# Conditioned linear-attention layer on one core: the last two turns of a software pipeline put in another order

## The chip, the cores and the metric

The kernel runs on one core of a Trainium2 chip. The metric is the device time of one execution in microseconds, the median of several runs. Names of engines are those of the profile: PE (TensorE, the matrix engine), PEld (its weight loads), DVE (VectorE), ACT (ScalarE), POOL (GpSimd), SP (the queue that issues loads and stores of x). PE writes PSUM only, and POOL works on SBUF only.

## The reference

Input x is 128 sequences of 64 tokens by 256 features in float32; there are 8 heads of 32. The softmax of q runs over a head's features, that of k over the tokens.

```python
xn = _ln(x, ln_w, ln_b)
q = xn @ Wq + bq
k = xn @ Wk + bk + (1.0 - src_mask) * -1000000.0
q = softmax(q.reshape(b, t, h, dh), axis=-1)
k = softmax(k.reshape(b, t, h, dh), axis=1)
v = ((xn @ Wv + bv) * src_mask).reshape(b, t, h, dh)
att = jnp.einsum('bnhd,bnhl->bhdl', k, v)
y = jnp.einsum('bnhd,bhdl->bnhl', q, att).reshape(b, t, d)
scale, shift = jnp.split((silu(emb) @ W_emb + b_emb)[:, None, :], 2, axis=2)
hh = _ln(y, ln2_w, ln2_b) * (1.0 + scale) + shift
hh = silu(hh) @ W_out + b_out
return x + hh
```

## The kernel before

The 8192 tokens are worked in G = 16 groups of 512 tokens (T = 4 tiles of 128 tokens, GB = 8 sequences). The features are C = 2 chunks of 128. Large products are split in float32r parts, high times high, high times low and low times high.

Each engine runs its own list of turns, `steps(engine, body)`: i = -1, 0, 1, 2 written out, the turns up to 14 in a hardware loop of two turns, and i = 15, 16, 17 written out. In turn i the engines work at up to four groups at once, by flags: N, the statistics and layer norm of x of group i+1; F, "front", K, Q and V of group i; B, attention and y of group i-1; O, the output of group i-2. Turn 15 has F, B, O; turn 16 has B (group 15) and O (group 14); turn 17 has only O (group 15). Within an engine, instructions start in the order of its list. Between engines, semaphores order them: each stage counts one up (`k_d`, `att_d`, `y_d`, `yhat_d`, ...), and who needs it waits for a count.

The steps of one group, with the lines of the profile:

- ACT's exp k (L400); PE transposes exp k into the banks `be` (L715, `exp_k_transposed`); ACT copies them to `e_k` (L389).
- ACT's exp q (L396); PE transposes it into the banks `bt` (L766); ACT copies that to `q_t` (L406).
- PE's attention, 128 small matmuls of `e_k` and `v_s` into `be` (L782); DVE's reciprocal of the sums (L596) and `kv` (L600).
- PE's y, 128 small matmuls of `kv` and `q_t` into all four banks of `by` (L802). `be` is banks 0 and 1 of `by`, `bt` its banks 2 and 3.
- DVE: reciprocal `rq` (L627), `y_s` (L631), statistics (L638, L641), two small ones (L644, L645); POOL: the power -0.5 (L340), a product (L342), the normalized y in place in `y_s` (L345; four tiles, in turn 16 two on POOL and two on ACT at L443).
- PE transposes the normalized y into `be` (L725, `y_transposed`); DVE scales it to `z_s` (L556), POOL adds the shift (L236; in turn 17 DVE); ACT's tanh `th` (L412); DVE's `h_s` = (th + 1) z (L609); ACT's rounded copy `h_hi` (L426); POOL's rest `h_lo` (L240; in turn 17 DVE).
- PE's output product, 24 matmuls of 256 columns into `bv` (lines 816 to 825; four of h_hi come before the wait for h_lo); DVE adds it to x (L656), in two halves; SP stores.

The profile gives the helper's line, L665, for all matmuls made by `mm`, so they are told apart by their tiles: `by<-v_s,e_k` is attention, `by<-kv,q_t` is y, `bv<-w_o_hi,h_hi` and its like the output product. In PE's turn 16 the order is: exp k of 15 transposed, y of 14 transposed, q of 15 transposed, attention of 15, y of 15, output product of 14. In turn 17: y of 15 transposed, output product of 15. The banks `bk_` hold K and then tiles 2 and 3 of the Q and V product; nothing writes them after turn 15.

Of the kernel before, what the change touches and what calls it, by code (L numbers as in the profile page):

```python
# [20 lines left out]
def build_layer(nc, x, cond_t, columns_in, b_qvk, mask_rows, wq, wk, wv, w_emb, w_out, b_out, out):  # L21
    fp32 = mybir.dt.float32
    f32r = mybir.dt.float32r
    ALU = mybir.AluOpType
# [3 lines left out]
    P = 128  # L28
# [16 lines left out]
    with ctx:  # L45
# [245 lines left out]
        def _(pool):  # L291
# [8 lines left out]

            def body(i, par, N, F, B, O):
# [149 lines left out]
        def _(dve):  # L451
# [99 lines left out]

            def z_scaled(g):
                for c in range(C):
# [4 lines left out]
                        be[c][:, :].rearrange("p (b s) -> p b s", s=SEQ),  # L558
# [6 lines left out]
            def body(i, par, N, F, B, O):  # L565
                if F:
# [22 lines left out]
                if B:  # L589
                    g = i - 1  # L590
                    wait(dve, att_d, g + 1)
                    wait(dve, kv_d, 2 * g)
                    sums = [be[e][:, 0:GB // 2 * C * AW].rearrange("p (b c n) -> p b c n", c=C, n=AW)
                            for e in range(2)]
                    for e in range(2):
                        nc.vector.reciprocal(rk[:, e, :, :], sums[e][:, :, :, DH]).then_inc(rk_d, 1)  # L596
                    wait(dve, y_d, g)
                    for e in range(2):
                        wait(dve, rk_d, 2 * g + e + 1)
                        nc.vector.tensor_tensor(  # L600
                            kv[:, e:GB:2, :, :], sums[e],
                            rk[:, e, :, :].unsqueeze(3).broadcast_to([P, GB // 2, C, AW]),
                            ALU.mult).then_inc(kv_d, 1)
                if O:
                    g = i - 2
                    for c in range(C):
                        wait(dve, th_d, 2 * g + c + 1)
                        wait(dve, hlo_d, 2 * g)
                        nc.vector.scalar_tensor_tensor(h_s[:, c, :], th[:, c, :], 1.0, z_s[:, c, :],  # L609
                                                       ALU.add, ALU.mult).then_inc(h_d, 1)  # L610
                    if last_step(i):
                        for c in range(C):
                            wait(dve, hhi_d, 2 * g + c + 1)
                            wait(dve, o_d, 2 * g)
                            h_low(nc.vector, c).then_inc(hlo_d, 1)
                if F:
                    q_tiles(i, par, (0, 1))
                if B:
# [44 lines left out]
        def _(pe):  # L663
# [55 lines left out]
            def y_transposed(g, B):  # L719
                wait(pe, yhat_d, 4 * g + 4)  # L720
                for c in range(C):
                    if B:
                        wait(pe, ek_d, 2 * g + c + 3)
                    for t in range(T):
                        last = nc.tensor.transpose(be[c][:, t * P:t * P + P], y_s[:, t, c * P:c * P + P],  # L725
# [3 lines left out]
            def body(i, par, N, F, B, O):  # L729
# [9 lines left out]
                if B:  # L739
                    exp_k_transposed(i - 1, par)  # L740

                for c in range(C):
# [15 lines left out]
                    if O and c == 0:  # L758
# [104 lines left out]
```

## Time and profile before

| | before |
|---|---|
| median of 3 runs | 356.78 us (354.89 to 357.75) |
| the profiled execution | 354.55 us |
| its span, first to last instruction | 352.7 us |
| PE busy | 326.3 us (93%) |
| DVE busy | 280.0 us (79%) |
| POOL busy | 193.3 us (55%) |
| ACT busy | 182.5 us (52%) |
| mean granted PE clock | 0.985 |

Times in the timelines are microseconds from the span's start. A timeline row is one instruction or several alike merged; in brackets stands how long the engine had sat idle before it, and who ended that wait. A PE matmul's time reaches from its start to a modelled end, and consecutive ones overlap, so their rate is read from starts. The granted clock is 1.00 at 2.4 GHz and 0.50 at 1.2 GHz. A steady turn takes about 20 us.

### The profile page before, as it was taken

The page shows a single profiled execution, that of the slowest core. Times are in us where ns is not written, and L with a number is a line of the kernel's source. Part 1 is how long each engine was busy: PE and PEld are TensorE (multiplying, and loading weights), DVE is VectorE, ACT ScalarE, POOL GpSimd, SP SyncE. Part 2 cuts the span into 40 slices and gives each one's busy share as a digit, 9 for nine tenths or more (in the row PEclk, how much of TensorE's full clock was granted, in tenths as well). Part 3 has the DMA queues.
Part 4 walks back from the last instruction along what each step waited for, and adds up shares of the span by engine and source line. Part 5 has one row for each costly group of instructions (what it writes and reads, how often), then busy time and mean ns, then how long its engine had stood idle before and what let it go on. Part 6 is the DMA issues. An engine that isn't in the chain of part 4 may idle for free.

```text
span 352.7 us, 14361 instructions
## 1 busy us (share of the span) xinstructions
PE 326.3 (93%) x5644; PEld 267.9 (76%) x5644; DVE 280.0 (79%) x749; ACT 182.5 (52%) x360; POOL 193.3 (55%) x244
## 2 busy tenths in 40 slices
PE   3799999999999999999999999999999999999736
PEld 2387868888787788788787788888788788888625
DVE  3777879698887969698887969698887969777672
ACT  0537547465455647465445647465545747453340
POOL 1221466467492937567492837567393837556520
PEclk9999999999999999999999999999999999999886
DMA  8920100301203030300203030200303010101011
GB/s 251 226 61 1 63 1 6 115 9 39 84 3 119 0 119 0 109 10 32 87 0 119 0 119 0 85 34 24 95 0 119 0 59 0 62 4 56 8 62 59
DMA packets 19818, 19.75 MB, mean 56 GB/s; under 512 B 1233, under 2 KB 19281, under 8 KB 19794
## 3 DMA queue, kind: packets, MB, share of 16 engines
q1 hardware_dynamic: 18144, 17.96, 16.6%
q10 hardware_dynamic: 1650, 1.45, 1.4%
q8 instruction: 17, 0.28, 0.3%
q14 instruction: 7, 0.06, 0.1%
HBM read 10.95 MB, written 8.39 MB: 55 GB/s over the span
## 4 chain that ended last, share of the span: by engine, by line
PE 47%; POOL 22%; issue 12%; DVE 11%; DMA 4%; DVEq 1%; POOLq 1%; ACT 1%; ACTq 0%
PE bk L665 19%; PE bv L665 14%; POOL h_lo L240 9%; PE by L725 4%; POOL xr L317 4%; PE by L715 3%; PE by L736 3%; POOL x_all L328 3%; PE by L665 3%; DVE kmax L578 3%; POOL xr L319 3%; DMA n_row<-n_lo 2%; DVE xstat L466 2%; POOL y_s L345 1%; DVE xmv L470 1%
## 5 line engine op out<-in xcount | busy, mean ns | idle before, releaser
L236 POOL TENSOR_TENSOR z_s<-z_s,mod_shift 128x512 f32<-128x512 f32 x30 | 30.7, 1044 | 68.7 <-DVE z_s L556 68.7
L400 ACT ACTIVATE k_t<-k_t 128x512 f32<-128x512 f32 x32 | 20.2, 631 | 64.7 <-DVE k_t L582 64.7
L383 ACT ACTIVATE xt_hi<-by 128x512 fp32r<-128x512 f32 x32 | 17.4, 597 | 46.6 <-PE by L736 46.6
L578 DVE TENSOR_REDUCE kmax<-bk 128x8 f32<-128x512 f32 x32 | 22.1, 690 | 23.8 <-PE bk L665 22.5
L240 POOL TENSOR_TENSOR h_lo<-h_s,h_hi 128x512 fp32r<-128x512 f32 x30 | 38.0, 1289 | 4.9 <-ACT h_hi L426 4.9
L665 PE MATMUL bv<-w_o_hi,h_hi 128*128 128x256 f32 x128 | 35.5, 296 | 4.5 <-ACT h_hi L426 4.5
L328 POOL TENSOR_TENSOR x_all<-x_all,bo_all 128x1024 f32 (+1 forms) x16 | 38.2, 2389 | 0.1
L345 POOL TENSOR_SCALAR y_s<-y_s,yr 128x256 f32<-128x256 f32 x62 | 33.9, 563 | 2.6 <-POOL yr L342 2.2
L665 PE MATMUL bv<-w_o_lo,h_hi 128*128 128x256 f32 x128 | 35.1, 294 | 0.0
L665 PE MATMUL bv<-w_o_hi,h_lo 128*128 128x256 f32 x128 | 28.6, 306 | 6.8 <-POOL h_lo L240 6.8
L656 DVE TENSOR_TENSOR x_all<-bv,x_all 128x512 f32 (+1 forms) x32 | 22.1, 691 | 14.9 <-PE bv L665 13.9
L432 ACT ACTIVATE xhat<-x_all,xr 128x256 f32 (+1 forms) x64 | 33.1, 592 | 1.1 <-POOL xr L321 1.1
L315 POOL TENSOR_SCALAR xr<-xmv 128x4 f32<-128x4 f32 x16 | 3.2, 198 | 52.1 <-DVE xmv L470 52.1
L665 PEld LDWEIGHTS bv<-w_o_hi,h_hi 128*128 128x128 f32 x128 | 25.8, 202 | 5.4 <-ACT h_hi L426 4.7
L665 PEld LDWEIGHTS by<-kv,q_t 32*64 32x64 f32 x2048 | 23.8, 131 | 7.7 <-issue 6.4
L665 PE MATMUL bk<-xt_hi,w_k_hi 128*128 128x512 f32 x64 | 28.6, 446 | 0.0
L665 PEld LDWEIGHTS bv<-w_o_hi,h_lo 128*128 128x128 f32 x128 | 21.0, 201 | 9.7 <-POOL h_lo L240 9.7
L665 PE MATMUL by<-kv,q_t 32*64 32x33 f32 x2048 | 25.7, 223 | 1.9 <-DVE kv L600 1.2
L665 PEld LDWEIGHTS bv<-w_o_lo,h_hi 128*128 128x128 f32 x128 | 25.8, 202 | 0.6
L569 DVE TENSOR_TENSOR xt_lo<-by,xt_hi 128x512 fp32r<-128x512 f32 x32 | 20.6, 685 | 6.2 <-ACT xt_hi L383 6.2
L665 PE MATMUL bk<-xt_hi,w_k_lo 128*128 128x512 f32 x64 | 25.3, 396 | 0.0
L582 DVE TENSOR_TENSOR k_t<-bk,kmax 128x512 f32<-128x512 f32 x32 | 22.1, 691 | 2.2
(104 smaller groups left out, 842.2 us busy)
## 6 DMA issues: line engine op xcount, KB each, us to landing
x_all<-in_x SPq DMA_DIRECT2D x16, 512.0 KB, 4.5
out<-x_all SPq DMA_DIRECT2D x15, 512.0 KB, 3.2
z_s<-in_w_emb ACTq DMA_DIRECT2D x1, 512.0 KB, 8.3
h_s<-in_w_emb ACTq DMA_DIRECT2D x1, 512.0 KB, 11.5
out<-x_all SPq DMA_DIRECT2D x2, 256.0 KB, 2.1
y_s<-in_wk SPq DMA_DIRECT2D x1, 256.0 KB, 3.1
q_t<-in_wq SPq DMA_DIRECT2D x1, 256.0 KB, 5.2
th<-in_cond_t ACTq DMA_DIRECT2D x1, 256.0 KB, 6.7
```

What stands on the lines that cost most here:

```text
L236: return eng.tensor_tensor(z, z, mod_shift[:, c, span(g, GB)].unsqueeze(2).broadcast_to([P, GB, SEQ]), ALU.add)
L240: return eng.tensor_tensor(h_lo[:, c, :], h_s[:, c, :], h_hi[:, c, :].bitcast(fp32), ALU.subtract)
L328: nc.gpsimd.tensor_tensor(xg, xg, bo_all[:, :].unsqueeze(1).broadcast_to([P, T, D]), ALU.add).then_inc(xb_d, 1)
L345: nc.gpsimd.tensor_scalar(y_s[:, t, :], y_s[:, t, :], yr[:, 1, t:t + 1], yr[:, 3, t:t + 1], ALU.mult, ALU.add).then_inc(yhat_d, 1)
L383: nc.scalar.activation(xt_hi[:, c, :], bt[c][:, :], ACT.Copy).then_inc(hi_d, 1)
L400: nc.scalar.activation(k_t[:, par, c, :], k_t[:, par, c, :], ACT.Exp).then_inc(kexp_d, 1)
L432: nc.scalar.activation(xhat[:, 1 - par, t, :], group_of(x_all, g)[:, :, t * D:t * D + D].rearrange("p g n -> p (g n)"), ACT.Identity, scal ...
L569: nc.vector.tensor_tensor(xt_lo[:, c, :], bt[c][:, :], xt_hi[:, c, :].bitcast(fp32), ALU.subtract).then_inc(lo_d, 1)
L578: nc.vector.tensor_reduce(out=kmax[:, c, :], in_=kk, axis=AX.X, op=ALU.max).then_inc(kmax_d, 1)
L582: nc.vector.tensor_tensor(k_t[:, par, c, :].rearrange("p (b s) -> p b s", s=SEQ), kk, kmax[:, c, :].unsqueeze(2).broadcast_to([P, GB, SEQ] ...
L656: nc.vector.tensor_tensor(xg, bv_[e][:, :], xg, ALU.add).then_inc(res_d, 1)
L665: return nc.tensor.matmul(dst, lhsT, rhs, start=start, stop=stop)
```

## The change

In the written-out turns 15 and 16 four things change place:

- PE transposes exp k of group 15 in turn 15, behind the Q and V product and ahead of the output product of group 13, in place of the start of turn 16.
- PE transposes y of group 14 behind the attention of group 15 in place of ahead of the q transposes, and into K's banks `bk_`; it waits for the last q_s of turn 15 (`qsub_d`), no longer for the copies of exp k. The attention waits for z_s of group 13 in place of 14.
- DVE does the reciprocals and kv of group 15 (`kv_scaled`) first in turn 16, ahead of z_s of 14; and h_s of group 14 (`h_product`) behind the statistics of y of 15 in place of ahead of the reciprocal of y.
- POOL does h_lo of group 14 (`h_lows`) behind the normalized y of 15 in place of ahead of the power.

The helpers `kv_scaled`, `h_product` and `h_lows` hold, unchanged, the lines that stood in the bodies. In the diff POOL's list comes first, then DVE's, then PE's.

```diff
+        def yt_bank(g):
+            return bk_ if isinstance(g, int) and g == G - 2 else be
...
-                if O and not last_step(i):
-                    g = i - 2
-                    for c in range(C):
-                        wait(pool, hhi_d, 2 * g + c + 1)
-                        wait(pool, o_d, 2 * g)
-                        h_low(nc.gpsimd, c).then_inc(hlo_d, 1)
+                if O and not last_step(i) and not last_y(i):
+                    h_lows(i - 2)
...
                     for t in range(T) if not last_y(i) else (0, 1):
                         nc.gpsimd.tensor_scalar(y_s[:, t, :], y_s[:, t, :], yr[:, 1, t:t + 1], yr[:, 3, t:t + 1],
                                                 ALU.mult, ALU.add).then_inc(yhat_d, 1)
+                if last_y(i):
+                    h_lows(i - 2)
...
-                        be[c][:, :].rearrange("p (b s) -> p b s", s=SEQ),
+                        yt_bank(g)[c][:, :].rearrange("p (b s) -> p b s", s=SEQ),
...
             def body(i, par, N, F, B, O):
+                if last_y(i):
+                    kv_scaled(i - 1, i)
...
+                if B and not last_y(i):
+                    kv_scaled(i - 1, i)
+                if O and not last_y(i):
+                    h_product(i - 2, i)
...
                     nc.vector.tensor_scalar(yr[:, 2, :], ymv[:, :, 0], -1.0, None, ALU.mult).then_inc(yve_d, 1)
+                if last_y(i):
+                    h_product(i - 2, i)
...
             def y_transposed(g, B):
                 wait(pe, yhat_d, 4 * g + 4)
+                if isinstance(g, int) and g == G - 2:
+                    pe.wait_ge(qsub_d, 4 * G)
                 for c in range(C):
-                    if B:
+                    if B and not (isinstance(g, int) and g == G - 2):
                         wait(pe, ek_d, 2 * g + c + 3)
...
-                if B:
+                if B and not last_y(i):
                     exp_k_transposed(i - 1, par)
...
-                    if O and c == 0:
+                    if O and c == 0 and not last_y(i):
                         y_transposed(i - 2, B)
...
-                    wait(pe, zs_d, 2 * g)
+                    wait(pe, zs_d, 2 * g - 2 if last_y(i) else 2 * g)
...
                     last.then_inc(att_d, 1)
+                    if last_y(i):
+                        y_transposed(i - 2, B)
...
                     qv_tile(i, 3)
+                    if isinstance(i, int) and i == G - 1:
+                        exp_k_transposed(i, 1 - par)
```

How the engines' lists stand before and after follows, from the built programs. The line numbers of the changed kernel differ (L715 is L732 there, L725 L744, L766 L785, L665 L682).

PE before, from the last matmuls of the output product of 13 at the end of turn 15 to the first of the output product of 14 in turn 16 (`k_t` is exp k, `v_s,e_k` attention, `kv,q_t` y):

```order
L665 MATMUL bv<-w_o_hi,h_lo 128x256 x2
L715 MATMUL by<-ident,k_t 128x128 x8
L725 MATMUL by<-ident,y_s 128x128 x8
L766 MATMUL by<-ident,q_s 128x128 x8
L665 MATMUL by<-v_s,e_k 32x33 x64
L665 MATMUL by<-kv,q_t 64x33 x64
L665 MATMUL bv<-w_o_hi,h_hi 128x256
```

The same place after:

```order
L682 MATMUL bv<-w_o_hi,h_lo 128x256 x2
L785 MATMUL by<-ident,q_s 128x128 x8
L682 MATMUL by<-v_s,e_k 32x33 x64
L744 MATMUL bk<-ident,y_s 128x128 x8
L682 MATMUL by<-kv,q_t 64x33 x64
L682 MATMUL bv<-w_o_hi,h_hi 128x256
```

The exp k transposes are gone from here (they stand now directly ahead of the output product of 13), and those of y stand between attention and y, into `bk`. Behind this piece nothing moves: the output product of 14 and then the transposes of y of 15.

DVE before, turn 16, from z_s of 14 to the residual of 14 (`rk` and `kv` of 15, `h_s` of 14, then y of 15):

```order
L556 TENSOR_TENSOR z_s<-by,mod_scale 128x512 x2
L596 RECIPROCAL rk<-by 128x8 x2
L600 TENSOR_TENSOR kv<-by,rk 128x4x66 x2
L609 SCALAR_TENSOR_TENSOR h_s<-th,z_s 128x512 x2
L627 RECIPROCAL rq<-by 128x32
L631 TENSOR_TENSOR y_s<-by,rq 128x512 x2
L638 BN_STATS ystat<-y_s 128x6 x4
L641 BN_AGGR ymv<-ystat 128x2 x4
L644 TENSOR_SCALAR yr<-ymv 128x4
L645 TENSOR_SCALAR yr<-ymv 128x4
L656 TENSOR_TENSOR x_all<-bv,x_all 128x512 x2
```

And after:

```order
L567 RECIPROCAL rk<-by 128x8 x2
L571 TENSOR_TENSOR kv<-by,rk 128x4x66 x2
L592 TENSOR_TENSOR z_s<-bk,mod_scale 128x512 x2
L642 RECIPROCAL rq<-by 128x32
L646 TENSOR_TENSOR y_s<-by,rq 128x512 x2
L653 BN_STATS ystat<-y_s 128x6 x4
L656 BN_AGGR ymv<-ystat 128x2 x4
L659 TENSOR_SCALAR yr<-ymv 128x4
L660 TENSOR_SCALAR yr<-ymv 128x4
L580 SCALAR_TENSOR_TENSOR h_s<-th,z_s 128x512 x2
L673 TENSOR_TENSOR x_all<-bv,x_all 128x512 x2
```

kv went ahead of z_s, and h_s from ahead of the reciprocal of y to behind the last of its statistics.

POOL before, its last rows (turn 16: shift of 14, h_lo of 14, power, product and two normalized tiles of 15):

```order
L236 TENSOR_TENSOR z_s<-z_s,mod_shift 128x512 x2
L240 TENSOR_TENSOR h_lo<-h_s,h_hi 128x512 x2
L340 TENSOR_TENSOR yr<-yr,neg_half 128x4
L342 TENSOR_TENSOR yr<-yr 128x4
L345 TENSOR_SCALAR y_s<-y_s,yr 128x256 x2
```

And after:

```order
L240 TENSOR_TENSOR z_s<-z_s,mod_shift 128x512 x2
L347 TENSOR_TENSOR yr<-yr,neg_half 128x4
L349 TENSOR_TENSOR yr<-yr 128x4
L352 TENSOR_SCALAR y_s<-y_s,yr 128x256 x2
L244 TENSOR_TENSOR h_lo<-h_s,h_hi 128x512 x2
```

h_lo is now the last that POOL does.

## Rows read from the trace of the kernel before

**Rows 1.** The page, part 4: shares of the span of the chain that ended last.

```profile
PE 47%; POOL 22%; issue 12%; DVE 11%; DMA 4%; DVEq 1%; POOLq 1%; ACT 1%; ACTq 0%
```

**Rows 2.** Timeline, 320 to 332 us: start, length, engine, line, operation, count [idle before <-releaser].

```profile
320.60 0.40 PE L665 MATMUL bv<-w_o_hi,h_lo 128*128 128x256 f32 x2
...
322.58 2.17 POOL L345 TENSOR_SCALAR y_s<-y_s,yr 128x256 f32<-128x256 f32 x4
...
323.00 1.03 PE L715 MATMUL by<-ident,k_t 128*128 128x128 f32 x8
323.20 0.69 DVE L656 TENSOR_TENSOR x_all<-bv,x_all 128x512 f32<-128x512 f32 x1 [0.25 <-PE bv L665]
323.63 1.08 ACT L389 ACTIVATE e_k<-by 128x512 f32<-128x512 f32 x2 [2.84 <-PE by L715]
324.61 1.15 ACT L396 ACTIVATE q_s<-q_s 128x512 f32<-128x512 f32 x2
...
324.81 1.09 PE L725 MATMUL by<-ident,y_s 128*128 128x128 f32 x8 [0.77 <-POOL y_s L345]
...
326.89 1.28 PE L665 MATMUL by<-v_s,e_k 64*32 64x33 f32 x128
...
328.21 0.28 DVE L596 RECIPROCAL rk<-by 128x8 f32<-128x8 f32 x2 [1.43 <-PE by L665]
...
329.35 0.43 PE L665 MATMUL by<-kv,q_t 32*64 32x33 f32 x18 [1.18 <-DVE kv L600]
...
330.52 1.44 PE L665 MATMUL by<-kv,q_t 32*64 32x33 f32 x110 [0.73 <-issue]
```

**Rows 3.** Timeline, 330 to 345 us, the same columns.

```profile
330.64 2.51 POOL L240 TENSOR_TENSOR h_lo<-h_s,h_hi 128x512 fp32r<-128x512 f32 x2 [2.32 <-ACT h_hi L426]
...
332.10 0.36 DVE L627 RECIPROCAL rq<-by 128x32 f32<-128x32 f32 x1 [1.60 <-PE by L665]
...
333.20 0.80 PE L665 MATMUL bv<-w_o_hi,h_lo 128*128 128x256 f32 x2 [0.43 <-POOL h_lo L240]
...
335.62 0.69 DVE L656 TENSOR_TENSOR x_all<-bv,x_all 128x512 f32<-128x512 f32 x1
...
335.86 1.02 POOL L340 TENSOR_TENSOR yr<-yr,neg_half 128x4 f32<-128x4 f32 x1 [2.72 <-DVE yr L645]
...
337.00 0.69 DVE L656 TENSOR_TENSOR x_all<-bv,x_all 128x512 f32<-128x512 f32 x1 [0.69 <-PE bv L665]
...
337.26 1.09 POOL L345 TENSOR_SCALAR y_s<-y_s,yr 128x256 f32<-128x256 f32 x2
...
338.41 1.09 PE L725 MATMUL by<-ident,y_s 128*128 128x128 f32 x8 [1.45 <-POOL y_s L345]
...
344.97 0.63 PE L665 MATMUL bv<-w_o_hi,h_lo 128*128 128x256 f32 x2
```

**Rows 4.** Chain of waits that ended last, its last stretch: start, length, engine, tile, line.

```profile
339.10 0.70 DVE z_s L556
...
343.95 5.50 PE bv L665 x24
...
349.48 0.69 DVE x_all L656
```

**Rows 5.** Timeline near 295 us; then line L319: count, ns min/median/max.

```profile
294.75 1.28 DVE L609 SCALAR_TENSOR_TENSOR h_s<-th,z_s 128x512 f32<-128x512 f32 x2
...
295.38 0.72 POOL L319 TENSOR_TENSOR xr<-xmv,xr 128x4 f32<-128x4 f32 x1
...
L319 POOL TENSOR_TENSOR xr<-xmv,xr x16: 199/669/718, 10.2 to 295.4; 128x4 f32<-128x4 f32 x16
```

**Rows 6.** Stretches of TensorE: from:to, length, busy (instructions), granted clock, DMA share, GB/s.

```profile
332.50:333.00 0.50, 0.27 (x2) 0.50 0.00 0
...
335.50:336.00 0.50, 0.50 (x5) 0.77 0.00 0
...
343.00:343.50 0.50, 0.00 (x0) 0.50 0.00 0
```

More of the change, by code:

```diff
@@ L299, in _, with h_lows @@
             pool.memset(v_s[:, :, :, :, DH:AW], 1.0).then_inc(pool_init, 1)
+            def h_lows(g):
+                for c in range(C):
+                    wait(pool, hhi_d, 2 * g + c + 1)
+                    wait(pool, o_d, 2 * g)
+                    h_low(nc.gpsimd, c).then_inc(hlo_d, 1)
             def body(i, par, N, F, B, O):
@@ L550, in q_tiles, with kv_scaled, h_product @@
                                             ALU.subtract).then_inc(qsub_d, 1)
+            def kv_scaled(g, i):
+                wait(dve, att_d, g + 1)
+                wait(dve, kv_d, 2 * g)
+                sums = [be[e][:, 0:GB // 2 * C * AW].rearrange("p (b c n) -> p b c n", c=C, n=AW)
+                        for e in range(2)]
+                for e in range(2):
+                    nc.vector.reciprocal(rk[:, e, :, :], sums[e][:, :, :, DH]).then_inc(rk_d, 1)
+                wait(dve, y_d, g)
+                for e in range(2):
+                    wait(dve, rk_d, 2 * g + e + 1)
+                    nc.vector.tensor_tensor(
+                        kv[:, e:GB:2, :, :], sums[e],
+                        rk[:, e, :, :].unsqueeze(3).broadcast_to([P, GB // 2, C, AW]),
+                        ALU.mult).then_inc(kv_d, 1)
+            def h_product(g, i):
+                for c in range(C):
+                    wait(dve, th_d, 2 * g + c + 1)
+                    wait(dve, hlo_d, 2 * g)
+                    nc.vector.scalar_tensor_tensor(h_s[:, c, :], th[:, c, :], 1.0, z_s[:, c, :],
+                                                   ALU.add, ALU.mult).then_inc(h_d, 1)
+                if last_step(i):
+                    for c in range(C):
+                        wait(dve, hhi_d, 2 * g + c + 1)
+                        wait(dve, o_d, 2 * g)
+                        h_low(nc.vector, c).then_inc(hlo_d, 1)
             def z_scaled(g):
@@ L588, in body @@
                     x_stats(i + 1, 1 - par)
-                if B:
[L590 to L615, printed above, removed]
+                if B and not last_y(i):
+                    kv_scaled(i - 1, i)
+                if O and not last_y(i):
+                    h_product(i - 2, i)
                 if F:
@@ L720, in y_transposed @@
                 wait(pe, yhat_d, 4 * g + 4)
+                if isinstance(g, int) and g == G - 2:
+                    pe.wait_ge(qsub_d, 4 * G)
                 for c in range(C):
-                    if B:
+                    if B and not (isinstance(g, int) and g == G - 2):
                         wait(pe, ek_d, 2 * g + c + 3)
                     for t in range(T):
-                        last = nc.tensor.transpose(be[c][:, t * P:t * P + P], y_s[:, t, c * P:c * P + P],
+                        last = nc.tensor.transpose(yt_bank(g)[c][:, t * P:t * P + P], y_s[:, t, c * P:c * P + P],
                                                    ident[:, :])
@@ L738, in body @@
                         last.then_inc(xt_d, 1)
-                if B:
+                if B and not last_y(i):
                     exp_k_transposed(i - 1, par)
```

## The prediction

> **What bounds the kernel now.** I read the page's shares of the chain first, then the timeline of the last 33 us by engine, then the chain of waits behind it, and last the granted clock in half-microsecond stretches. Over the whole span the chain that ended last lies on TensorE for 47% and on POOL for 22% [rows 1]; in the steady loop the change touches nothing. It touches three engines' orders in the turns i = 15, 16 and 17, and only the time from about 320 us on can move. There TensorE is no longer full. It waits 0.77 us for POOL's normalized y of group 14 before that is transposed, 1.18 us for DVE's kv of group 15, and 0.73 us in the midst of the y matmuls for nothing that the profile names [rows 2]. Then DVE makes y of group 15 and its statistics, POOL the power and half of the normalized y, and TensorE transposes it at 338.41 after idling 1.45 us for POOL [rows 3]. Between those, the output product of group 14 is hidden: its h_lo is ready at 333.15, and the last residual that depends on it starts at 337.00 [rows 3]. From 339.10, DVE's first product on the transposed y of group 15, the rest is one chain without slack, up to the last residual at 349.48 and the last store [rows 4].
>
> So the number that decides is when DVE can start that product of group 15 (339.10 before). Two paths lead to it: **path Y** (attention, kv, y, statistics, power, normalized y, transposes), which decides today, and **path O** (h_product of 14, h_hi, h_lo of 14, output product of 14), which ends earlier today, because TensorE runs the output product of 14 ahead of the transposes of 15, and DVE the residual of 14 ahead of that product. The change keeps both of these orders.
>
> **Path Y, step by step.** Moving the eight exp k transposes ahead of the output product of group 13 costs that product what they take. Sixteen transposes take from 324.81 to 326.89, so 1.04 us for eight [rows 2]. The product then ends, and the q transposes start, at 323.00 + 1.04 = 324.04 us. Their input is there: ACT stood idle for the exp k transposes (2.84 us in front of its copies of them [rows 2]); with these done near 321.2 the copies end before 322.3; DVE's q_s stands ahead of the residual of 323.20 in its order, so the second half of the exp (1.15 us for both halves [rows 2]) ends before 323.8. Attention starts at 324.04 + 1.04 = 325.08 in place of 326.89: **1.81 us earlier**, which is the wait of 0.77 and the y transposes of 14 (1.04) that no longer stand ahead. It takes 1.28, to 326.36. DVE's reciprocal goes from 328.21 to 326.40 (DVE is free: its residual, 1.04 later, ends at 324.93). The time from there to the first y matmul was 329.35 - 328.21 = 1.14, so these may start at 327.54. In that gap stand now the y transposes of 14, 326.36 to 327.40, hidden with 0.14 to spare; were they to take longer, the excess would lie on path Y. They write K's banks, whose last reader (q_s of tiles 2 and 3) is done before 323.20; the new wait costs nothing. On DVE the products of 14 (z_s, 1.3 us) now follow kv, and end near 328.8, ahead of 330.29, when y is complete: also hidden. The unnamed 0.73 us I keep, since the matmuls in front of it are the same in number. So y of 15 is complete at 332.10 - 1.81 = 330.29, and POOL's power starts at 335.86 - 1.81 = 334.05. Here path Y is still 1.81 us ahead, and if it decided, the kernel would end that much earlier.
>
> **Path O, which the change lengthens.** Before, h_product of 14 stood on DVE ahead of the reciprocal of y, and POOL's h_lo started at 330.64, ahead of the power of 15 [rows 3]. Now h_product starts where the first residual stood (335.62 - 1.81 = 333.81 [rows 3]), and POOL's h_lo stands behind the power, the product and the two normalized tiles. Those end at 337.26 + 1.09 = 338.35 before, so at 336.54.
>
> One price more lies on POOL. DVE's two h_s products (1.28 us for the pair) run from 333.81 to 335.09, just when the power starts. The trace has such a meeting: POOL's product of xr and mean takes 199 ns at best and 669 ns in the median, and the one at 295.38 took 0.72 us, its end 0.07 us behind DVE's h_s pair of 294.75 to 296.03 [rows 5]. The excess, 669 - 199 = 0.47 us, is my price for the power. Its bounds are 0 (the power has read its few numbers first) and 335.09 - 334.05 = 1.04 (it waits for the whole pair). The Trainium skill, "SBUF — State Buffer", section "Who interferes with whom", states that a DVE instruction with two SBUF inputs contends with a GpSimd one that reads SBUF, and that the loser fully blocks. The trace agrees in the row at 295.38. By that rule taken for both products the price would be the upper bound, and the forecast 0.57 us later.
>
> Then: POOL's tiles end at 336.54 + 0.47 = 337.01; h_lo starts 0.04 later (a gap such as those between its instructions) and takes 2.51 [rows 3], to 339.56; TensorE takes it up 0.05 later (333.20 against 333.15), at 339.61. From that first h_lo pair to the last residual twenty matmuls follow. The trace has this stretch at three speeds: 2.60 us (320.60 to 323.20 [rows 2]) at the full clock, 3.80 (333.20 to 337.00 [rows 3]) where the granted clock is 0.50 for the first 2.5 us and then rises [rows 6], and 4.51 (344.97 to 349.48 [rows 3, 4]) at 0.50 nearly throughout. Half the full clock is 1.2 in place of 2.4 GHz. Before the second, TensorE had idled for 0.43 us and little before; before the third, for 4.5 us, from 339.5 to 343.95. Now it idles from about 330.2 until h_hi comes near 335.8, does four matmuls and idles again for h_lo. That is nearest to the third, so I take 4.51: last residual of 14 at 344.12. It takes 0.69, and with 0.02 of gap the first product of 15 starts at 344.83. The transposes of 15, started some 0.2 us ahead of that residual as at 323.00, have their first half done within it.
>
> **The sum.** 344.83 - 339.10 = **5.73 us later**, and nothing behind it changes: same instructions, same wait of TensorE, same store. On the profiled execution, 354.55 us (span 352.7), this gives 360.3. That execution is the lowest of the four known times; the timed runs were 354.89, 356.78 and 357.75, and the mean of all four is 355.99. I set the forecast at 355.99 + 5.6 = 361.6 us, 0.1 off for a clock that may come back earlier. A measurement can tell about 1% (3.6 us) from no change, and this is 1.35% of the median.
>
> **Rivals.**
> - *A: path O decides, at a slow clock* (forecast, chance 0.70): +4.8 to +6.8 us. It spans the contention's bounds, -0.47 to +0.57, and up to 0.5 for a late y transpose or one more unnamed stall.
> - *B: path O decides, and the clock comes back during the product of 14* (0.17): as in the mixed stretch 3.80 for 4.51, or somewhat better: +3.8 to +5.0, so about 360. For it speaks the rise at 335.5 to 336.0 after less than 3 us of matmuls [rows 6]; against it, the long idle before, and that the last product shows 0.50 from its start on.
> - *C, not slower: TensorE's clock.* If the work left in the last 16 us kept TensorE at 2.4 GHz, the product of 14 would take 2.60 for 4.51 (-1.91), and the last product, 5.53 us from 343.95 to 349.48, would fall by at least as much for the same twenty matmuls and about 0.5 for its first four: 5.73 - 1.91 - 2.4 = +1.4 us, 357.4, which is within 1%. If the 0.73 us stall also went, +0.7. It decides only if the clock is up when h_lo arrives; 5 us of idling ahead speak against it. Chance 0.07.
> - *D: path Y gives nothing* (0.06): the y transposes or z_s in front of path Y eat the 1.81 us. Then POOL's chain starts as before, and the whole is +7.5 us, 363.5.
>
> **How the numbers follow.** The range reaches from B on the lowest known run's level (355 + 3.8 = 358.8) to A's upper end near the median's (356.8 + 6.8 = 363.6); C and D and a drift of the level stay outside. Faster than 1% would need C and more that no row offers: 0.02. Within 1%: C, and a part of B that ends at +3.6 or less: 0.13. Slower by over 1%: 0.85.
>
> **What would show it.** In the changed kernel's trace: exp k transposes ahead of the output product at 320.1; attention near 325.1; y transposes into bk right behind it, with hardly a wait for kv; POOL's power near 334.0, and longer than its 1.02 us; h_lo ending near 339.6, which TensorE waits for over 2 us after four matmuls; the transposes of group 15 near 343.9 without any wait for y, directly behind the product of 14; and 10.4 us from DVE's first product of 15 to its last residual, as before. Wrong would be: a wait for POOL's y_s in front of the last transposes (path Y decides after all), a product of 14 in 2.6 us, or an attention that starts no earlier.

## The result and the profile after

| | before | after |
|---|---|---|
| median | 357.26 us (354.89 to 358.59, 4 runs) | 364.65 us (362.81 to 364.95, 4 runs) |
| the profiled execution | 354.55 us | 362.81 us |
| its span | 352.7 us | 361.0 us |
| PE busy | 326.3 us (93%) | 330.2 us (91%) |
| mean granted PE clock | 0.985 | 0.967 |

The ratio of the medians is 1.021, with a 95% interval of 1.015 to 1.026: the change made the kernel slower by about 2%, as forecast in direction, but by more, and 364.65 us lies above the range of 358.8 to 363.6.

The page of after, the heads of its parts and the chain, which answers to [rows 1]:

```profile
span 361.0 us, 14361 instructions
...
PE 330.2 (91%) x5644; PEld 270.8 (75%) x5644; DVE 280.5 (78%) x749; ACT 182.5 (51%) x360; POOL 193.4 (54%) x244
...
PE 49%; POOL 21%; issue 11%; DVE 10%; DMA 4%; DVEq 1%; POOLq 1%; ACT 0%; ACTq 0%
```

The chain lies on PE for 49% of a longer span. The timeline of after where [rows 2] stand for before:

```profile
322.05 1.03 PE L732 MATMUL by<-ident,k_t 128*128 128x128 f32 x8
...
326.76 1.29 PE L682 MATMUL by<-v_s,e_k 64*32 64x33 f32 x128
...
328.09 0.28 DVE L567 RECIPROCAL rk<-by 128x8 f32<-128x8 f32 x2 [1.41 <-PE by L682]
...
329.23 0.43 PE L682 MATMUL by<-kv,q_t 32*64 32x33 f32 x18 [0.16 <-DVE kv L571]
...
331.18 1.44 PE L682 MATMUL by<-kv,q_t 32*64 32x33 f32 x110 [1.51 <-issue]
```

All times here are later by a start that has nothing to do with the change (below). POOL's h_lo of group 13, ahead of everything that moved, starts at 316.87 us in the trace of before and 1.92 us later in that of after:

```profile
316.87 2.54 POOL L240 TENSOR_TENSOR h_lo<-h_s,h_hi 128x512 fp32r<-128x512 f32 x2 [2.56 <-ACT h_hi L426]
```

```profile
318.79 2.55 POOL L244 TENSOR_TENSOR h_lo<-h_s,h_hi 128x512 fp32r<-128x512 f32 x2 [2.55 <-ACT h_hi L435]
```

With 1.92 taken off, attention starts at 324.84 (before 326.89) and the first y matmul at 327.31 (329.35), with a wait for kv of 0.16 in place of 1.18 us. That half works as forecast. Then PE stops for 1.51 us in the midst of the y matmuls, where it stopped for 0.73 before [rows 2]. The stretch of [rows 3]:

```profile
332.75 0.36 DVE L642 RECIPROCAL rq<-by 128x32 f32<-128x32 f32 x1 [2.38 <-PE by L682]
...
336.28 1.29 DVE L580 SCALAR_TENSOR_TENSOR h_s<-th,z_s 128x512 f32<-128x512 f32 x2
...
336.52 1.33 POOL L347 TENSOR_TENSOR yr<-yr,neg_half 128x4 f32<-128x4 f32 x1 [4.62 <-DVE yr L660]
...
338.24 1.09 POOL L352 TENSOR_SCALAR y_s<-y_s,yr 128x256 f32<-128x256 f32 x2
...
339.29 2.48 POOL L244 TENSOR_TENSOR h_lo<-h_s,h_hi 128x512 fp32r<-128x512 f32 x2
...
341.83 0.79 PE L682 MATMUL bv<-w_o_hi,h_lo 128*128 128x256 f32 x2 [2.32 <-POOL h_lo L244]
...
346.26 1.83 PE L744 MATMUL by<-ident,y_s 128*128 128x128 f32 x8
346.50 0.69 DVE L673 TENSOR_TENSOR x_all<-bv,x_all 128x512 f32<-128x512 f32 x1 [1.80 <-PE bv L682]
347.35 0.69 DVE L592 TENSOR_TENSOR z_s<-by,mod_scale 128x512 f32<-128x512 f32 x1 [0.16 <-PE by L744]
...
357.73 0.69 DVE L673 TENSOR_TENSOR x_all<-bv,x_all 128x512 f32<-128x512 f32 x1 [1.80 <-PE bv L682]
```

POOL's y of 15 is ready at 339.33, and its transposes start only at 346.26, directly behind the output product of 14, which waited 2.32 us for h_lo. Y was ready for 6.9 us. The last residual starts at 357.73, 10.38 us behind the first z_s at 347.35, just as before (349.48 - 339.10 [rows 4]). The granted clock in the stretches of after, for [rows 6] (from:to, length, busy, clock, DMA share, GB/s):

```profile
334.50:335.00 0.50, 0.00 (x0) 0.50 0.00 0
...
346.50:347.00 0.50, 0.50 (x4) 0.50 0.00 0
...
348.00:348.50 0.50, 0.09 (x1) 1.00 0.70 238
...
352.00:352.50 0.50, 0.30 (x1) 0.50 0.00 0
```

PE ran at 1.2 GHz from 334.5 to 347.5, which holds the whole product of 14 and most of the transposes of 15 behind it, and again in the last product.

So that runs with different starts can be compared, I read two distances in each trace: **head**, from the start of POOL's h_lo of group 13 to DVE's first z_s of group 15 (22.23 us before, 28.56 after), and **end**, from that to the last residual (10.38 in both). Their sum rose by 6.33 us; the medians rose by 7.4 with an interval of 5.4 to 9.4.

### The profile page after: what moved, and what is told of

Same layout as the page of the kernel before. It is cut to its first block, busy times and chain, and to the rows that moved or that the text cites. A ratio compares the mean times of both kernels' runs of the same rounds, so it can differ in the third digit from the quotient of the medians.

```text
span 361.0 us, 14361 instructions
## 1 busy us (share of the span) xinstructions
PE 330.2 (91%) x5644; PEld 270.8 (75%) x5644; DVE 280.5 (78%) x749; ACT 182.5 (51%) x360; POOL 193.4 (54%) x244
## 4 chain that ended last, share of the span: by engine, by line
PE 49%; POOL 21%; issue 11%; DVE 10%; DMA 4%; DVEq 1%; POOLq 1%; ACT 0%; ACTq 0%
PE bk L682 19%; PE bv L682 16%; POOL h_lo L244 10%; PE by L744 4%; POOL xr L328 4%; PE by L732 4%; PE by L755 3%; PE by L682 3%; POOL x_all L339 3%; DMA n_row<-n_lo 3%; POOL xr L330 3%; DVE kmax L616 3%; DVE xstat L475 2%; DVE xmv L479 1%; DMA mask_r<-in_mask_rows 1%
## 5 line engine op out<-in xcount | busy, mean ns | idle before, releaser
L682 PE MATMUL bv<-w_o_hi,h_hi 128*128 128x256 f32 x128 | 36.3, 302 | 9.8 <-ACT h_hi L435 9.8
L682 PE MATMUL bv<-w_o_hi,h_lo 128*128 128x256 f32 x128 | 29.1, 311 | 8.6 <-POOL h_lo L244 8.6
L682 PE MATMUL bv<-w_o_lo,h_hi 128*128 128x256 f32 x128 | 35.7, 297 | 0.0
L682 PEld LDWEIGHTS bv<-w_o_hi,h_hi 128*128 128x128 f32 x128 | 26.3, 205 | 10.8 <-ACT h_hi L435 10.2
L682 PEld LDWEIGHTS bv<-w_o_hi,h_lo 128*128 128x128 f32 x128 | 21.4, 206 | 11.6 <-POOL h_lo L244 11.6
L682 PEld LDWEIGHTS by<-kv,q_t 32*64 32x64 f32 x2048 | 23.9, 131 | 7.5 <-issue 7.1
L682 PE MATMUL bk<-xt_hi,w_k_hi 128*128 128x512 f32 x64 | 29.1, 455 | 0.0
L682 PE MATMUL by<-kv,q_t 32*64 32x33 f32 x2048 | 25.8, 223 | 1.7 <-issue 1.5
L682 PEld LDWEIGHTS bv<-w_o_lo,h_hi 128*128 128x128 f32 x128 | 26.4, 206 | 0.6
L682 PE MATMUL bk<-xt_hi,w_k_lo 128*128 128x512 f32 x64 | 25.8, 402 | 0.0
L421 ACT ACTIVATE th<-z_s 128x512 f32<-128x512 f32 x32 | 18.6, 632 | 14.0 <-DVE z_s L240 10.2
```

The lines of the kernel that those rows point to most:

```text
L421: nc.scalar.activation(th[:, c, :], z_s[:, c, :], ACT.Tanh, scale=0.5).then_inc(th_d, 1)
L682: return nc.tensor.matmul(dst, lhsT, rhs, start=start, stop=stop)
```

## The experiments

Each row's time is compared with the kernel before, run beside it on the same chip: 358.24, 357.81 and 358.64 us on the three chips of the experiments (medians of 19 runs each), 357.26 for the row of after. So ratios can be compared, and absolute times of different rows less well. A table of all first, the edits and expectations below it. Head, end and stop come from one trace of each kernel. In the three kernels with a busy start (the last three rows) the stop in y comes behind 119 of its 128 matmuls, in all others behind 18.

| run | head | end | PE's stop in y | first matmul on emb | time against before (95%) |
|---|---|---|---|---|---|
| before | 22.23 | 10.38 | 0.73 | 20.00 | |
| before, once more | 22.68 | 9.83 | 0.92 | 23.45 | 1.001 (0.998 to 1.004) |
| after | 28.56 | 10.38 | 1.51 | 21.87 | 1.021 (1.015 to 1.026) |
| after, once more | 28.29 | 10.35 | 1.23 | 23.83 | 1.011 (1.002 to 1.020), 2 runs |
| h_lo of 14 on DVE | 23.86 | 9.62 | 0.37 | 23.03 | 1.007 (1.004 to 1.010) |
| h put back | 22.45 | 10.30 | 0.94 | 22.10 | 0.996 (0.993 to 1.000) |
| late h alone | 29.71 | 9.93 | 0.95 | 22.78 | 1.019 (1.014 to 1.024) |
| store of 13 held | 27.08 | 9.75 | 0.67 | 21.20 | 1.013 (1.008 to 1.017) |
| y of 15 transposed first | 20.95 | 9.78 | 0.73 | 22.91 | 0.998 (0.995 to 1.002) |
| before, PE kept busy | 22.38 | 8.29 | 0.68 | 23.98 | 0.998 (0.995 to 1.002) |
| h put back, PE kept busy | 21.44 | 8.28 | 1.26 | 21.43 | 0.989 (0.982 to 0.996) |
| the same, busy start too | 21.81 | 8.28 | 1.07 | 20.54 | 0.988 (0.983 to 0.994) |
| before, busy start | 25.13 | 10.37 | 0.74 | 19.96 | 1.003 (0.999 to 1.007) |
| all of it, store held | 21.50 | 8.28 | 1.62 | 20.10 | 0.984 (0.981 to 0.988) |

### h_lo of group 14 on DVE

```diff
-                if last_step(i):
+                if last_step(i) or last_y(i):
                     for c in range(C):
                         wait(dve, hhi_d, 2 * g + c + 1)
                         wait(dve, o_d, 2 * g)
                         h_low(nc.vector, c).then_inc(hlo_d, 1)
...
-                if last_y(i):
-                    h_lows(i - 2)
```

> The changed kernel with one edit: the two h_lo of group 14 are made by DVE right behind its h_s of group 14, not by POOL behind the normalized y. I measure from the start of POOL's h_lo of group 13 to DVE's first z_s of group 15: 22.23 us before (316.87 to 339.10), 28.56 after (318.79 to 347.35). Theory O (the output product of 14, which waits for h_lo in POOL's queue, holds up the transposes of 15): h_lo is ready some 2.8 us earlier, the product runs on behind its four first matmuls, and the distance falls by about 2.6, to 25.9; kernel about 1% slower than before in place of 2%. Rival Y (the y path, its stall and the slow clock hold the transposes up): no change, 28.5.

The head fell by 4.70 us, from 28.56 to 23.86, more than the 2.6 expected. 1.14 of that is PE's stop, 0.37 for 1.51 us. Of the rest 2.8 us is h_lo, and the product of 14 had part of the full clock: its two residuals stand 1.86 us apart, 2.49 in after. In the time, +0.7% in place of +2.1%. That h_lo in POOL's queue is what the product waits for is shown; rival Y falls.

### h of group 14 put back

```diff
-                if O and not last_step(i) and not last_y(i):
+                if O and not last_step(i):
                     h_lows(i - 2)
...
-                if last_y(i):
-                    h_lows(i - 2)
...
-                if O and not last_y(i):
+                if O:
                     h_product(i - 2, i)
...
-                if last_y(i):
-                    h_product(i - 2, i)
```

> The changed kernel with h_s of group 14 (DVE) and h_lo of group 14 (POOL) put back to where they stood before; exp k early, kv first and y of 14 into K's banks stay. Theory O: h_lo is done before POOL's power again, so the loss goes: the distance from POOL's h_lo of 13 to the first z_s of 15 is 21.5 to 22.4 us (before 22.23, after 28.56), the kernel within 0.3% of before. Rival Y (the new attention and store order costs the time): most of the 6.3 us stays, distance over 26.

All of the loss is gone: head 22.45 us (expected 21.5 to 22.4), time 0.996 (0.993 to 1.000). Its timeline, POOL's h_lo, PE's first pair on it, the power, the transposes of 15 and z_s:

```profile
334.62 1.27 POOL L244 TENSOR_TENSOR h_lo<-h_s,h_hi 128x512 fp32r<-128x512 f32 x1
...
335.94 0.80 PE L678 MATMUL bv<-w_o_hi,h_lo 128*128 128x256 f32 x2 [0.67 <-POOL h_lo L244]
...
337.16 1.02 POOL L347 TENSOR_TENSOR yr<-yr,neg_half 128x4 f32<-128x4 f32 x1 [1.27 <-DVE yr L658]
...
340.37 1.46 PE L740 MATMUL by<-ident,y_s 128*128 128x128 f32 x8
...
341.43 0.69 DVE L590 TENSOR_TENSOR z_s<-by,mod_scale 128x512 f32<-128x512 f32 x1
```

h_lo ends at 335.89 and no longer stands behind the power; but the product of 14, at half the clock, still ends behind the normalized y (339.65), and so eats what exp k, kv and the transposes in K's banks gain.

### The late h alone

The edit is made on the kernel before; the lines that move are those of `h_product` and `h_lows`, and the loops in them are left out here.

```diff
-                if O:
+                if O and not last_y(i):
                     g = i - 2
...
                     nc.vector.tensor_scalar(yr[:, 2, :], ymv[:, :, 0], -1.0, None, ALU.mult).then_inc(yve_d, 1)
+                if last_y(i):
+                    g = i - 2
...
-                if O and not last_step(i):
+                if O and not last_step(i) and not last_y(i):
                     g = i - 2
...
                                                 ALU.mult, ALU.add).then_inc(yhat_d, 1)
+                if last_y(i):
+                    g = i - 2
```

> The kernel before with only the other half: h_s of group 14 behind the statistics of y of 15 on DVE, h_lo of 14 behind the normalized y on POOL. Nothing is gained ahead of the statistics, so theory O expects more than the whole change cost: h_lo ends near 341.2, the product's last residual starts 4.6 later, the distance from h_lo of 13 to the first z_s of 15 is 29.9 us (before 22.23), the kernel 2.1 to 2.4% slower. Rival Y: the late h costs little, distance below 25.

Head 29.71 us, 0.2 from the expectation and above that of the whole change; time +1.9%, a little under the 2.1 to 2.4% expected. The late h costs 7.5 us alone (29.71 - 22.23). The two halves together show the change as a loss of 7.5 and a gain of 1.15 us (29.71 - 28.56); the stop was 0.95 here and 1.51 there, and with equal stops the gain would be 1.7. Here the clock also came back at the end of the product of 14 (residuals 2.29 us apart for 2.49, z_s 0.61 behind the second for 0.85); with that equal too my estimate is 2.1, near the 2.05 us by which attention came earlier in after.

### The store of group 13 held

```diff
             def store(g):
+                if isinstance(g, int) and g == G - 3:
+                    sp.wait_ge(y_d, G)
                 wait(sp, res_d, 2 * g + 2)
```

> The changed kernel with one edit: SP sends the store of group 13 only once y of group 15 is complete. In the trace of after, the unnamed stop of PE inside the y matmuls of 15 grew from 0.73 to 1.51 us, and the packet of the instruction queue just ahead of it ran among the packets of that store (328.64 us), while before it ran alone (328.05). Theory S (PE waits for instructions, whose fetch queues behind the store's packets): the stop falls back to about 0.7 us and the distance from h_lo of 13 to the first z_s of 15 from 28.56 to 27.8. Rival (the stop has to do with the new order of matmuls): it stays at 1.5 us.

The DMA queues of before in 328.0 to 328.3 us, and of after in 328.0 to 329.2 us (queue, packets, MB, share of 16 engines):

```profile
q8 instruction: 1, 0.02, 20.5%
```

```profile
q1 hardware_dynamic: 382, 0.38, 93.1%
q8 instruction: 1, 0.02, 5.2%
```

With the store held the stop was 0.67 us, as expected, and the head 27.08, lower than the 27.8 expected: 0.84 of the 1.48 is the stop, the rest the clock that came back within the product of 14 (its residuals 2.09 us apart for 2.49). But the other traces don't bear theory S out. With the packet among the store's the stop was 1.51, 1.23, 1.26 and 0.94, but also 0.73 (y of 15 transposed first) and 0.37 us (h_lo on DVE); with the packet alone it was 0.73, 0.92, 0.95, 0.68 and 0.67; and the last kernel below, which holds the store too, stops for 1.62 us. So the stop varies by a microsecond between executions. It is longer where the store runs beside it by 0.2 us in the mean (1.01 against 0.79 over these eleven), and that the store does this is not shown.

What the traces do show is that the stop follows the packet. In all fourteen PE goes on 2.3 to 3.2 us behind the start of a packet of 16 KB, which fits a wait for instructions. In after that time was 2.53 us and in before 2.52, so the packet took no longer there; but it started 1.89 us behind the start of attention, in before 1.11 and in the six other traces with after's attention and y order and no busy start 0.9 to 1.1, whether the store ran beside it or not. The late packet is the 0.78 us by which the stop of after exceeds that of before. Why it was late in that one execution is open.

### y of group 15 transposed ahead of the product of 14

```diff
                 if last_y(i):
                     h_product(i - 2, i)
+                    z_scaled(i - 1)
+                    h_product(i - 1, i + 1)
...
+                if last_y(i):
+                    y_transposed(i - 1, False)
                 if O:
                     g = i - 2
...
+        def h_of(g):
+            return (xt_hi, xt_lo) if isinstance(g, int) and g == G - 1 else (h_hi, h_lo)
```

> The changed kernel, with h_lo of 14 left late on POOL, but PE transposes y of 15 ahead of the output product of 14, and DVE does z_s, h_s and h_lo of 15 ahead of the two residuals of 14; h_hi and h_lo of 15 go to the free buffers of x transposed, so that they need not wait for the product of 14. Theory O (the late h_lo hurts only because the transposes of 15 and z_s stand behind the product of 14): the distance from POOL's h_lo of 13 to the first z_s of 15 falls from 28.56 to about 21.6 us, and the last residual is no longer 10.4 us behind that but some 13, since the product of 15 now waits for that of 14; kernel within 0.5% of before. Rival Y (the y path itself became late): distance above 25.

Here the late h_lo stays. POOL's h_lo of 14 and the transposes of 15:

```profile
340.87 2.50 POOL L248 TENSOR_TENSOR h_lo<-h_s,h_hi 128x512 fp32r<-128x512 f32 x2
340.96 1.97 PE L750 MATMUL by<-ident,y_s 128*128 128x128 f32 x8 [6.76 <-POOL y_s L356]
```

The transposes start 0.05 us behind POOL's last tile of y, beside h_lo and not behind it: head 20.95 us, the shortest of all. So it is the order of PE and DVE in the last turn, product of 14 first, that made the late h_lo costly. The second half of the expectation was wrong: the last residual stands 9.78 us behind z_s, not 13. The clock came back between 346.5 and 347 us, and the last product, at 2.4 GHz, took 3.11 us to the last residual in place of 5.53 [rows 4]; that is 2.4 of the 3.2 us. The sum of both distances, 30.73, is 1.9 us under before (1.8 under before once more), and the time did not move beyond the noise (0.995 to 1.002, or 1.9 us less to 0.7 us more).

### PE kept busy

The extra matmuls write a bank that nobody reads afterwards, so their results are thrown away.

```diff
+            def keep_busy(n):
+                wait(pe, zs_d, 2 * (G - 2) + 2)
+                for _ in range(n):
+                    mm(bk_[0][:, :], w_qv_hi[:, 0, 0:P], xt_hi[:, 0, :], True, True)
...
+                if last_step(i):
+                    keep_busy(18)
                 if O:
                     g = i - 2
                     wait(pe, hhi_d, 2 * g + 2)
```

> The kernel before, with 18 extra matmuls of 512 columns, results thrown away, on PE behind the last transposes, where PE idled 4.45 us ahead of the last output product. Theory C (that idling costs the last product its clock): granted clock stays at 1.00, the product's 24 matmuls take about 3.1 us to the last residual in place of 5.5, kernel 0.7% faster than before. If in a run the clock is low already when they start, they take twice as long and delay the product by up to 3 us. Rival: the product takes 5.5 us whatever precedes it, no change.

With 8 more ahead of the product of 14, on the kernel with h put back:

> The kernel with h_s and h_lo of 14 put back (exp k early, kv first, y of 14 into K's banks) and extra matmuls, results thrown away: 8 ahead of the output product of 14 and 18 ahead of that of 15. Theory C with path Y: the product of 14 at the full clock no longer holds up the transposes of 15, distance from h_lo of 13 to the first z_s of 15 about 21.5 us (22.45 without the extra ones), last product 3.1 us in place of 5.5: 1.2% faster than before. Rival: the clock stays low in both, same time as without them, 0.4% faster.

Of the kernel with h put back and PE kept busy, the last transposes, the extra matmuls, the first of the last product and the last residual:

```profile
339.20 1.09 PE L740 MATMUL by<-ident,y_s 128*128 128x128 f32 x8 [1.09 <-POOL y_s L352]
340.05 4.43 PE L678 MATMUL bk<-xt_hi,w_qv_hi 128*128 128x512 f32 x18
...
344.76 0.39 PE L678 MATMUL bv<-w_o_hi,h_hi 128*128 128x256 f32 x1 [0.27 <-ACT h_hi L433]
...
348.18 0.69 DVE L669 TENSOR_TENSOR x_all<-bv,x_all 128x512 f32<-128x512 f32 x1 [0.68 <-PE bv L678]
```

The last product takes 3.42 us from first matmul to last residual, where it took 5.53 [rows 4], and in this kernel nothing is in front of the last transposes but POOL's y (they waited 1.09 us for it). Head 21.44 us, 0.8 under before: some of the y path's gain appears once the product of 14 is out of the way. Time 0.989. What the 8 matmuls and the 18 give each alone on this kernel was not run. On the kernel before, the same 18 matmuls shorten the end to 8.29 us, 2.1 less than in the trace of before and 1.5 less than in before once more (9.83), whose clock came back by itself within the last product. The time moved by 0.2% only, not the expected 0.7%; the interval, 1.8 us less to 0.7 more, doesn't hold the 2.1 us and does hold the 1.5. Whether that is why is open.

### The start, and all together

```diff
+            for _ in range(8):
+                mm(be[0][:, 0:P], ident[:, :], ident[:, :], True, True)
             pe.wait_ge(fold_ready, C)
...
+                            pe.wait_ge(weights_ready, 1)
+                            for _ in range(12):
+                                mm(be[0][:, 0:D], w_k_hi[:, 0, 0:P], w_k_hi[:, 1, :], True, True)
                             pe.wait_ge(n_rows_in, 32)
-                            pe.wait_ge(weights_ready, 1)
```

> As the run with 8 and 18 extra matmuls, and 20 more at the program's start: 8 ahead of the first product and 12 ahead of K of group 0. In the traces so far the first matmul on the embedding starts at 20.0 us (before), 21.9, 23.0, 22.1, 22.8 and 21.2 us, later where K of group 0 ran at a granted clock of 0.5, and all behind it is late by as much. Theory C: with PE busy from the start K of group 0 runs at the full clock in every execution, that matmul starts at 20.0, the spread of the runs shrinks and the median falls by another 1.5 to 2.5 us, to about 1.7% faster than before. Rival: the first clock has to do with something else, no change against the run without these 20.

> The kernel before with the 20 extra matmuls at the start alone, results thrown away. In nine traces the first matmul on the embedding starts between 20.0 and 24.0 us, as K of group 0 ran at the full or the half clock, and the profiled execution of before was the one at 20.0. Theory L (my level was too low because that start decides 0 to 4 us of every run): it starts near 20.5, the median falls by 1.5 to 2.5 us, 0.4 to 0.7%, and the runs spread over less than 2 us. Rival: the level has another cause, same median and spread (355 to 360) as before.

> The kernel before once more, for a second trace. Theory L: the first matmul on the embedding starts later than 20.0 us (as in seven of eight other traces) and the whole execution is longer by the same, while the distance from POOL's h_lo of 13 to the first z_s of 15 stays at 22.2 (+-0.3) and the stop at 0.7. Rival: the tail itself varies by a microsecond or more.

> The changed kernel once more, for a second trace. If the tail is as the first trace shows it, the distance from POOL's h_lo of 13 to the first z_s of 15 is 28.0 to 28.6 us (28.56), the unnamed stop of PE 1.3 to 1.6 us, POOL's power 1.33 us, and the first matmul on the embedding starts anywhere from 20 to 24. If the stop was chance, it is 0.7.

> h_s and h_lo of 14 put back, extra matmuls at the start and in the last two turns (results thrown away), and the store of group 13 held until y of 15 is complete. Theory S: PE's unnamed stop in the y matmuls of 15, 1.26 and 1.07 us in the two runs without the held store, falls to 0.7, all of it on the y path, which decides here: distance from h_lo of 13 to the first z_s of 15 about 21.2 us (21.44 and 21.81 without), kernel 1.3% faster than before, the fastest so far. Rival: the stop stays, 1.2% as without.

The start first. A matmul of K of group 0 in the trace of before, and in that of after:

```profile
16.84 0.39 PE L665 MATMUL bk<-xt_hi,w_k_lo 128*128 128x512 f32 x1
...
20.00 0.60 PE L665 MATMUL by<-th,z_s 128*128 128x128 f32 x4
```

```profile
17.51 0.63 PE L682 MATMUL bk<-xt_hi,w_k_lo 128*128 128x512 f32 x1
...
21.87 0.60 PE L682 MATMUL by<-th,z_s 128*128 128x128 f32 x4
```

The same product took 0.23 us from start to start at the full clock and 0.43 at half of it. That makes about 1.5 of the 1.87 us; K began 0.37 us later (16.45 for 16.08), and what stands behind is late by the sum. Over the traces of kernels that are alike up to turn 15 the first matmul on the embedding starts at 20.0 to 24.0 us; the profiled execution of before is the lowest, and none of the ten others came under 21.2. Taken once more, before had it at 23.45, and POOL's h_lo of group 13 at 321.08, 4.21 us later than in the first trace:

```profile
321.08 2.54 POOL L240 TENSOR_TENSOR h_lo<-h_s,h_hi 128x512 fp32r<-128x512 f32 x2 [2.57 <-ACT h_hi L426]
```

Its head is 22.68 us (0.18 above the 22.2 +- 0.3 that was expected), its stop 0.92, its end 9.83, and its profiled time 358.65 us, the level of the 19 runs and 4.10 above the first trace. So this execution at the usual level differs from the one I summed on by its part ahead of group 13, and hardly by its tail (-0.10 us). After, once more: 23.83, head 28.29 and power 1.33 us as expected, the stop 1.23 just under the 1.3 to 1.6 expected. Its median, over two runs, is 4.1 us above before (0.8 to 7.2).

The extra matmuls did bring the first matmul on the embedding to 20.54, 19.96 and 20.10 us. But in the median they brought nothing: 353.43 against 353.17 us without them (runs 352.99 to 354.31 against 352.98 to 356.14), and on the kernel before +0.3%, with eight runs from 357.6 to 361.8 us and two at 363.5. There the trace shows what took their place, a new stop of PE inside the attention of group 15:

```profile
330.63 0.27 PE L665 MATMUL by<-v_s,e_k 64*32 64x33 f32 x9 [2.13 <-issue]
...
334.73 0.52 PE L665 MATMUL by<-kv,q_t 32*64 32x33 f32 x9 [0.74 <-issue]
```

The head of this kernel is 25.13 us. With the 54 instructions added ahead, PE's stops stand at another place of its program in all three traces with a busy start: besides the one behind 119 of the y matmuls, 2.13 us inside attention here, and 0.78 and 0.46 us ahead of the transposes of y of 14 in the two others. So the start is shown to move 1 to 4 us of an execution, most of it by the clock; that a busy start brings the medians down by as much is not shown, since they did not fall.

All together with the store held: 352.67 us, 0.984 of before (0.981 to 0.988), the lowest time of all here, faster than before and after. Head 21.50 for the 21.2 expected, and the stop did not shrink (1.62, so theory S's expectation failed here). Against the two busy kernels without the held store (0.988 and 0.989, on another chip) the intervals overlap, so that holding the store gives anything is not shown.

## Why the prediction was right and wrong

The mechanism was right: path O, not path Y, decides, by PE's order (the product of 14 ahead of the transposes of 15) and POOL's (h_lo behind the normalized y). The slower direction, the wait of PE for h_lo (2.32 us; "over 2 us"), the transposes directly behind the product without a wait for y, and the unchanged 10.4 us of the end all came as written. The experiments bear it out: with h put back the loss goes, the late h alone makes all of it, and with the transposes of 15 ahead of the product the late h_lo costs nothing. Two sizes were off: the level, and the unnamed stop in the sum.

The measured 364.65 us lies 3.06 above 355.99 + 5.6. Of that, 1.27 is the level (357.26 for 355.99), 0.13 what I took off the sum, 0.60 the sum (6.33 for 5.73), and 1.06 that the medians rose by 7.39 and the two distances by 6.33; the last is within the interval of 5.4 to 9.4, and no trace explains it. The level alone would not have saved the range: its upper end on the right median, 357.26 + 6.8 = 364.06, is still 0.6 short.

**The level.** "I set the forecast at 355.99 + 5.6 = 361.6 us". This is the first step that failed, and the largest. It is only 4.8 above the median of 356.78 that a change of 5.73 would be seen from. The three runs and one trace of which I took the mean stood low: the median of before is 357.26 us over four runs, and 357.81 to 358.64 over 19 runs each in the experiments. The profiled execution I summed on was one whose K of group 0 ran at the full clock, which none of the ten other traces with that start did throughout. 357.26 + 5.73 would have been 363.0. The sum should have stood on the median, and the range should have taken in that a single trace's start can be up to 4 us early.

**The sum of 5.73.** It came out at 6.33 in the first pair of traces; after once more against before once more it is 28.29 - 22.68 = 5.61 in the head and 6.13 with the end. Term by term, in the first pair with 1.92 taken off:

- Attention 1.81 us earlier: it was 2.05. The q transposes started at 325.80 - 1.92 = 323.88 for 324.04, and attention 0.96 us behind them for 1.04.
- "The unnamed 0.73 us I keep, since the matmuls in front of it are the same in number": 1.51 and 1.23 us. This is the other step that failed: the term with the largest error, +0.78. The number of matmuls in front does not fix it: it varies from 0.37 to 1.26 us in other traces with as many in front, and follows the packet of instructions; y of 15 was complete 1.27 us earlier than before (332.75 - 1.92 = 330.83 against 332.10), not 1.81.
- The power's meeting with DVE's h_s, +0.47: it took 1.33 us for 1.02, +0.31, and 1.32 to 1.34 in five more traces with this order, while the four with h put back show 1.02. The POOL instruction starts 0.24 us behind the h_s pair's start and ends 0.28 us behind the pair's end. It was neither free nor blocked for the whole pair (1.05 us from its start). The Trainium skill, "SBUF — State Buffer", section "Who interferes with whom", calls contention for the ports that VectorE and GpSimd share an exclusive lock, and says, of VectorE's 2-port modes, that whoever issues first holds them for its whole instruction and the other blocks. Read for the pair as one, that is over three times the price measured; read for the first product alone (its 0.69 us end 0.45 behind the power's start) it is an estimate of 0.45. The measured 0.31 lies below both, and nearer the second.
- The product of 14 at 4.51 us from first h_lo pair to last residual: 4.67, all at half the clock, as chosen. Rival B's clock came back within it in three other runs (residuals 1.86, 2.09 and 2.29 us apart with h_lo on DVE, the store held and the late h alone), where the head was shorter for it.
- z_s behind the residual, 0.71: it was 0.85, since the eight transposes took 1.83 us at half the clock and z_s waited 0.16 for them. I had said that their first half would be done within the residual.

+0.30 up to the first h_lo pair (the stop's 0.78, less 0.24 of attention, 0.16 of the power and some hundredths in the gaps), +0.16 and +0.14 make the 0.60.

Rival C, not slower by the clock, did not happen, though two experiments show that it holds as a mechanism: with PE kept busy, the last product falls by 2.1 us. Rival D, in which path Y gives nothing, has its 7.5 us near the rise of the medians (7.4) by luck: y was complete 1.27 us earlier. The chance of 0.13 for "within 1%" counts a part of rival B at +3.6 or less, which B's own +3.8 to +5.0 doesn't have.

## What to carry to other kernels

Before moving a step behind another on one engine's list, look for who in another engine's list stands behind its consumer: here the h_lo moved by POOL was hidden only because the product on it ended ahead of the transposes. Changing both orders, or neither, took the loss away (0.998 and 0.996 of before); a time clearly under before came only with PE kept busy as well (0.989). Where two paths lead to one point, the gain of the one is worth nothing until the other is shortened too. And a forecast in absolute time belongs on the median of runs, since one trace can be the luckiest execution by up to 4 us; with small effects compare a distance inside the traces.

## What the runs showed of the hardware

- PE's clock fell to half after a stretch of idling (332.6 to 338.3 us in after, down from 334.5 on) and what followed up to 347.5 stayed there; 26 matmuls whose results are thrown away kept it at 1.00 and made an output product of 24 matmuls 3.42 us long in place of 5.53.
- PE stops for 0.4 to 1.6 us in the y matmuls of 15, and goes on 2.3 to 3.2 us behind the start of a 16 KB packet of the instruction queue; with 54 instructions more at the program's start one trace has such a stop inside attention, 2.13 us long, so extra instructions far ahead can undo a gain at the end.
- POOL's power of 128x4 takes 1.02 us alone and 1.32 to 1.34 beside a pair of DVE products with two inputs in SBUF, in all six traces with that meeting.
